# Graph attention layer: rows of 128 words in the gathered table, and the sources' part of the logits made on VectorE from the fetched rows

## What is computed

```python
xp = (x @ W).reshape(N, H, C)                      # H = 8, C = 16
a_src = jnp.einsum('nhc,hc->nh', xp, att_src)
a_dst = jnp.einsum('nhc,hc->nh', xp, att_dst)
e = leaky_relu(a_src[src] + a_dst[dst], 0.2)
m = segment_max(e, dst)
ex = exp(e - m[dst])
alpha = ex / (segment_sum(ex, dst)[dst] + 1e-16)
out = segment_sum(xp[src] * alpha[:, :, None], dst).reshape(N, 128) + bias
```

## Time and profile before

| | us |
|---|---|
| median of three runs | 10769.82 (10767.44 to 10773.94) |
| profiled execution, device time | 10778.69 |
| span of the profiled execution | 10776.9 |
| edge loop of the last layer, first to last merge (195 turns) | 2214.85 |

### The profile page before, as it was taken

The page is one execution under the profiler, slowest core; times in us unless marked ns, Lnnn a source line. Parts: engine busy times, 40 slices in busy tenths (PEclk is TensorE's granted clock), DMA queues, the critical chain, the costliest instruction groups (busy, mean ns, idle before and its releaser), DMA issues. The chain is left out here.

```text
span 10776.9 us, 275696 instructions
## 1 busy us (share of the span) xinstructions
PE 7528.6 (70%) x88315; PEld 6740.6 (63%) x88351; DVE 6269.2 (58%) x21527; ACT 2636.6 (24%) x7285; POOL 6069.2 (56%) x5927
## 2 busy tenths in 40 slices
PE   5994999997999997633333343899982566666665
PEld 4884989895898895333333333788881455555553
DVE  7995666664666666311111126677766566666666
ACT  3552222222222223200000002111111333333333
POOL 1332555552555552377777760677760777777773
PEclk7887999998999998855555566999996666666665
DMA  1005555553555555411111123333332111111113
GB/s 40 0 0 131 133 131 132 132 133 110 131 132 133 130 133 148 168 52 52 52 52 52 52 56 97 109 110 109 110 99 73 47 49 49 49 49 49 50 49 69
DMA packets 826148, 930.48 MB, mean 86 GB/s; under 512 B 135365, under 2 KB 720557, under 8 KB 825709
## 3 DMA queue, kind: packets, MB, share of 16 engines
q1 hardware_dynamic: 640390, 537.10, 17.2%
q0 software_dynamic: 185216, 386.21, 15.9%
q10 hardware_dynamic: 487, 6.55, 0.2%
HBM read 801.28 MB, written 134.46 MB: 87 GB/s over the span
## 5 line engine op out<-in xcount | busy, mean ns | idle before, releaser
L475 POOL DMA_INDIRECT ring<-att_table,idx x1592 | 1766.2, 1109 | 501.3 <-issue 455.0
L475 POOL DMA_INDIRECT ring<-rel_table,idx x1568 | 1486.5, 948 | 486.9 <-issue 477.2
L542 PE MATMUL psum<-sel,ring 128*128 128x128 f32 x3136 | 725.3, 425 | 1267.5 <-DMA ring<-rel_table,idx 1267.5
L1168 PE MATMUL psum<-state,ring 128*128 128x128 bf16 x24420 | 1511.8, 220 | 41.6 <-DVE ring L1115 34.1
L1122 DVE TENSOR_SCALAR state<-iota_row,state 128x128 f32<-128x128 f32 x5684 | 1530.1, 348 | 0.0
L542 PEld LDWEIGHTS psum<-sel,ring 128*128 128x128 f32 x3136 | 677.8, 328 | 1315.6 <-issue 1315.6
L1168 PEld LDWEIGHTS psum<-state,ring 128*128 128x128 bf16 x24420 | 1374.1, 98 | 152.2 <-issue 52.1
L1101 POOL DMA_INDIRECT ring<-gcn_table,idx x812 | 781.1, 962 | 747.9 <-ACT idx L1146 624.1
L1101 POOL DMA_INDIRECT ring<-rows,idx x812 | 781.2, 962 | 736.8 <-ACT idx L1146 612.9
L1346 POOL DMA_INDIRECT state<-hyp_table,state x980 | 962.7, 982 | 337.1 <-issue 281.3
L1182 PE MATMUL psum<-state 64*128 64x128 f32 x16240 | 1125.7, 282 | 0.3 <-DVE state L1122 0.2
(11 more groups left out here) (407 smaller groups left out, 13467.7 us busy)
## 6 DMA issues: line engine op xcount, KB each, us to landing
state<-xparts SPq DMA_DIRECT2D x814, 192.0 KB
state<-drow SPq DMA_DIRECT2D x814, 160.0 KB
rel_table<-tout SPq DMA_DIRECT2D x98, 512.0 KB, 2.6
ring<-xparts SPq DMA_DIRECT2D x199, 192.0 KB
ring<-srow SPq DMA_DIRECT2D x199, 192.0 KB
ring<-rows SPq DMA_DIRECT2D x70, 448.0 KB
ring<-att_table,idx POOLq DMA_INDIRECT x1592
ring<-rel_table,idx POOLq DMA_INDIRECT x1568
```

The costliest lines, as they stand in the source:

```text
L475: pool.indirect_dma_start(out=ring[:, u, k, 0:width], out_offset=None, in_=table, in_offset=bass.IndirectOffsetOnAxis(ap=idx[:, u, k:k + 1 ...
L542: last = nc.tensor.matmul(psum[:, u % 2, 0:WIN], ring[:, u, k, 0:D], sel[:, u % 2, k, :], start=(k == 0), stop=(k == K - 1))
L1168: last = nc.tensor.matmul(rowsP[v][:, j * P:(j + 1) * P], reach[v][:, t, j * P:(j + 1) * P], xwin[v][:, t, i, :], start=(t + i == 0), stop ...
```

## The change

The table in HBM has rows of 128 words; the stores leave the 8 logits of each row out, and a gather fetches 128 words per edge. `att_src` is loaded once more, flat and on all partitions (`att_s`), with one more DMA in the prologue. A new step on VectorE, `source_logits`, waits for the landing of a group, multiplies the 8 x 128 words per partition by `att_s` into `weighted`, waits for that product, and sums it over the 16 channels of each head into words 128 to 135 of the ring's slot. ScalarE's `stage_logits` waits for this sum (`slog`) where it waited for the landing. In VectorE's loop the step for group n+3 stands at the end of turn n, behind group_max(n+2); for groups 0, 1 and 2 it stands ahead of the loop.

```diff
-        att_table = nc.dram_tensor("att_table", (TILES * P, ROW5), F32, kind="Internal").ap()
+        att_table = nc.dram_tensor("att_table", (TILES * P, D), F32, kind="Internal").ap()
+        att_s = sb("att_s", [P, D])
+        weighted = sb("weighted", [P, K, D])
@@ prologue, sync engine (and the waits for "copied" go from 26 * 16 to 27 * 16)
+                sp.dma_start(att_s[:, :], att_src.rearrange("h c -> (h c)").partition_broadcast(P)
+                             ).then_inc(sem("copied"), 16)
@@ project, sync engine
-                                sp.dma_start(rows_of(to, b), tiles(tout[:, u, 0:BT * w], w)
+                                sp.dma_start(rows_of(to, b), tiles(tout[:, u, 0:BT * w], w)[:, :, 0:D]
@@ attention_pass
-                stage_index = gather_engines(block, att_table, srcT, ROW5, AHEAD,
+                stage_index = gather_engines(block, att_table, srcT, D, AHEAD,
@@ scalar engine (the calls lose their count in the same way)
-                    def stage_logits(n, u, count):
-                        act.wait_ge(sem(f"g{u}"), count)
+                    def stage_logits(n, u):
+                        act.wait_ge(sem("slog"), n + 1)
@@ vector engine
+                    def source_logits(n, u, landed):
+
+                        dve.wait_ge(sem(f"g{u}"), landed)
+                        if not isinstance(n, int) or n > 0:
+                            dve.wait_ge(sem("slog"), n)
+                        nc.vector.tensor_tensor(
+                            weighted[:, :, :], ring[:, u, :, 0:D], att_s[:, :].unsqueeze(1).to_broadcast([P, K, D]),
+                            ALU.mult).then_inc(sem("weighed5"), 1)
+                        dve.wait_ge(sem("weighed5"), n + 1)
+                        nc.vector.tensor_reduce(
+                            ring[:, u, :, D:ROW5], weighted[:, :, :].rearrange("p k (h c) -> p k h c", c=CH),
+                            axis=AX.X, op=ALU.add).then_inc(sem("slog"), 1)
@@ edge_logits
                         dve.wait_ge(sem("atedge"), n + 2)
+                        dve.wait_ge(sem("slog"), n + 1)
@@ ahead of the loop and at the end of each turn
+                    source_logits(0, 0, 16 * K)
                     select(0, 0)
@@
+                    source_logits(1, 1, 16 * K)
                     select(1, 1)
@@
                     group_max(1)
+                    source_logits(2, 2, 16 * K)
@@
                             group_max(n + 2)
+                            source_logits(n + 3, (u + 3) % RING,
+                                          it * (16 * K) + (16 * K if u < RING - 3 else 32 * K))
```

More of the change, by code:

```diff
@@ L213, in gnn_kernel @@
                      "ex", "msg", "summedE", "newrow", "newT", "wback",
-                     "below", "selb", "vstage", "vT", "bstage", "runmax", "runT", "runlast", "nodemax", "mg"):
+                     "below", "selb", "vstage", "weighed5", "slog", "vT", "bstage", "runmax", "runT", "runlast", "nodemax", "mg"):
             sem(name)
@@ L271, in _ @@
                 act.wait_ge(sem("load"), 12 * 16)
-                act.wait_ge(sem("copied"), 26 * 16)
+                act.wait_ge(sem("copied"), 27 * 16)
                 act.wait_ge(padded, 4 * 16)
@@ L355, in _ @@
                                           ALU.mult, ALU.add))
-                dve.wait_ge(sem("copied"), 26 * 16)
+                dve.wait_ge(sem("copied"), 27 * 16)
                 for r in range(RELS):
@@ L373, in _ @@
                 pe.wait_ge(sem("pool"), 7)
-                pe.wait_ge(sem("copied"), 26 * 16)
+                pe.wait_ge(sem("copied"), 27 * 16)
                 pe.wait_ge(sem("fin"), 1)
@@ L2235, in _ @@
                     logit_window(base_of(0))
-                    stage_logits(0, 0, 16 * K)
+                    stage_logits(0, 0)
                     starts_out(0)
@@ L2239, in _ @@
                     sel_out(0)
-                    stage_logits(1, 1, 16 * K)
+                    stage_logits(1, 1)
                     starts_out(1)
@@ L2248, in _ @@
                     sel_out(1)
-                    stage_logits(2, 2, 16 * K)
+                    stage_logits(2, 2)
                     with act.Fori(0, NG // RING) as it:
@@ L2272, in _ @@
                             sel_out(n + 2)
-                            stage_logits(n + 3, (u + 3) % RING,
-                                         it * (16 * K) + (16 * K if u < RING - 3 else 32 * K))
+                            stage_logits(n + 3, (u + 3) % RING)
                 @block.vector
```

## The result

The kernel after takes 11048.79 us (median of four runs, 11040.32 to 11062.78) against 10768.63 us: 280 us more, a ratio of 1.0261 with a 95% interval of 1.0243 to 1.0279. The profiled execution has a span of 11061.0 against 10776.9, 284 us more; at 11062.78 us it is the slowest of the four, 14 us above their median.

The account below looks back on a forecast made before the run. GpSimd, issuing gathers without a pause, bound the kernel at 11.358 us a turn. The longer ring adds 243 us and the two ends 2.5 each: 248, so 11027 us profiled, 11018 median; range 10960 to 11120.

Parts of the forecast that it names:

- Rows of 128 words cost and bring nothing: Table stores and gathers: gathers keep 0.943 us, stores gain 1.4 us at the very most, taken as 0.
- The step's own length: source_logits on VectorE: product 1.225 us, sum 1.212 us, 0.03 us ahead of each, 2.50 us together.
- The ring: Last layer's edge loop: dependences across VectorE, TensorE and ScalarE set the turn, 8.75 + 3.86 = 12.61 us against 11.358.
- the way from L2491 to L2471: From the matmuls' end through group_max, product, sum and ScalarE's copies to TensorE's turn_logits, one after the other: 3.86 us.
- the rest of the ring: Edge loop's dependent work without TensorE's wait ahead of turn_logits: 11.358 - 2.608 = 8.750 us a turn.
- TensorE's clock: Edge loop: at the 1.2 GHz level ring work is 9.13 us; all turns there would add 74 us, giving 11092.
- GpSimd second: Edge loop: GpSimd's turn 12.0 us, 0.6 below the ring's 12.61; rival that it stays last, 11095 us, chance 0.13.
- three holds of 0.68 us each: GpSimd's gathers, held under three long two-SBUF-input VectorE instructions a turn: 9.98 + 2.03 = 12.0 us.
- The ends: Outside the loop's turns: 2.5 us behind the first landing and 2.5 us ahead of the last copy.
- VectorE held in turn by a gather under way: Rival, messages and product: gathers under way block VectorE, 0.7 us a turn, 13.3 us, 11155 us; chance 0.04.
- The step hidden in TensorE's wait: Rival, edge loop: step fits TensorE's 2.608 us idle; about 10775 us, or 10900 with one more hold; chance 0.05.
- The row width as the cause of long gathers: Rival, gathers: GpSimd's floor becomes 10.0 us but the ring still gives 12.6; 10505 with a hidden step; chance 0.02.

Follow-up runs that it names:

- the second run with att_s in PSUM: The kernel after with att_s copied once to a free PSUM bank, run again off the chip that stretched every kernel: 11075.71 us, ratio 1.0266 to the kernel before.
- the step with wide rows: The kernel after with rows of 136 words stored and fetched again, the step overwriting the fetched logits: 11050.1 us, ratio 1.0262 to the kernel before.
- the early place: The kernel after with source_logits moved on VectorE from behind group_max to ahead of messages: 10823.83 us, ratio 1.0052 to the kernel before.
- select's row in PSUM: The kernel before with the row of indices that select reads copied once to a free PSUM bank: 10581.42 us, ratio 0.9825 to the kernel before.
- the kernel with both PSUM edits: The kernel before with select's row of indices and the edges' weights for messages in PSUM: 10549.09 us, ratio 0.9776 to the kernel before.
- the rows alone: The kernel before with rows of 128 words in table and gathers and no step on VectorE, output not the reference's: ratio 1.0004 to the kernel before.

## Why the prediction was right

**What bounds the kernel before.** Right: GpSimd's gathers with their holds. Taking away first select's and then both gave 1.75% and 2.24%.

**Rows of 128 words cost and bring nothing.** Right: 1.0004.

**The step's own length.** The product 1.225 us as forecast, the sum 1.220 against 1.212: 2.45 us and 0.06 for the two starts.

**The ring.** Right in mechanism: the 12.61 us forecast came out as 12.777. The difference, 0.17 us or 33 us in all, is most of the 36 us by which the 11027 for the profiled execution fell short of 11063. Half is in the way from L2491 to L2471, 3.950 us against 3.86: in half of the turns VectorE pauses 0.19 us between group_max and the product (19.5 us in 98 cases, above), which the earlier trace rows couldn't show. The other half is in the rest of the ring, 12.777 - 3.950 = 8.827 against 8.750. There I had named TensorE's clock, and the granted clock over the loop went from 0.64 to 0.59. The traces with the same ring bear it out in part. The way is the same in all, 3.95 to 3.96 us; the rest is 8.83 us at 0.59 (the kernel after), 8.75 at 0.61 (the second run with att_s in PSUM) and 8.65 at 0.63 (the step with wide rows). Turns that run at 0.50 throughout, the 1.2 GHz level, have a rest of 9.15 us on average in the kernel before and after alike, near the 9.13 of the prediction; the kernel after has 45 of them and the step with wide rows 17. So the size of the rest goes with the clock of the execution that happened to be profiled, and the 12.618 us of the step with wide rows, which fall on the forecast, owe it in part to the two errors of 0.1 us cancelling. No run sets the clock by itself.

**GpSimd second.** Right in rank: it waits for its indices, and a product that holds nothing leaves the time alone. Its turn of 8 x (1.170 + 0.305) = 11.8 us is near the 12.0 of the sum, and it idles 1.0 us a turn where I had 0.6. But three holds of 0.68 us each are not what came. Per turn the product's are worth 0.85 us, those of messages 0.84 and those of select 0.14; their sum, 1.8 us, is near the 2.03 of the forecast by luck. A held gather ends 0.8 us after VectorE's instruction, so a hold is worth anything from nothing to 1.05 us by where the gather begins under it. That didn't matter after the change, where GpSimd isn't last, and it is why the early place was better than I expected and select's row in PSUM too. The price of the sum, taken as 0, is right: in the second run with att_s in PSUM 198 gathers begin under it, half of them in its first 0.27 us, and all but one, begun in its last 0.01 us, take their usual time.

**The ends.** The first merge comes 8.1 us later. 4.1 of it arose ahead of the pass (its first gather starts at 8375.6 against 8371.5), where the change has next to nothing; the same point lies at 8396.5 in the kernel with both PSUM edits, which has nothing new there either, and between 8371.5 and 8398.7 in all undisturbed traces, so I take it for scatter. The other 3.9 are against 2.5 forecast; that the products for groups 1 and 2 add the rest is not shown. At the pass's end the forecast 2.5 us is absent. The last copy:

```profile
L2211 ACT ACTIVATE tout<-ring x199: 256/256/257, 8389.4 to 10916.0; 128x64 f32<-128x64 f32 x199
```

It starts 7.9 us after the last merge against 8.5 before (10631.80 in the earlier trace rows, the last merge at 10623.26). GpSimd is ahead there now, as in the loop, so the step takes the place of the wait for the last landing and isn't added to it.

**The rivals.** VectorE held in turn by a gather under way: no. The 199 products lie between 1.224 and 1.227 us, but only 34 of them begin under a gather. The kernel with select's row in PSUM says more: 192 of its 197 messages begin under one, last 1.224 to 1.226 us, and start 0.03 us after the weights like the others. The step hidden in TensorE's wait: that wait grew instead. The row width as the cause of long gathers: no, by the rows alone.

## What to carry to other kernels

A wait of 2.6 us on one engine is not room for 2.5 us of work on another: write down what has to follow what from the end of that wait backwards, and put the new step where its engine is idle and where what follows it on the ring has time to spare. Here the same instructions cost 2.6% behind group_max and 0.5% ahead of messages. And if GpSimd issues gathers without a rest, look first at what VectorE runs beside them: one operand moved to PSUM was worth 1.75%.

## What the runs showed of the hardware

A gather is held by one of these 128x1024 VectorE instructions with both inputs in SBUF if it begins while that one runs, and ends some 0.8 us after it: 1.97 us under the product above. An instruction of the same length with one input in PSUM holds none (0.94 us at 8609.06), nor does the reduction with its one input in SBUF (0.94 at 8610.31). A gather that began 0.07 us before such an instruction isn't held (9508.85), and VectorE's instruction is neither lengthened nor made to wait by it (192 messages of 1.224 to 1.226 us, above).

The Trainium skill ("SBUF — State Buffer", Who interferes with whom) says that on this chip a reduction never contends with GpSimd and that an instruction with two SBUF inputs does with one that reads SBUF. The trace agrees, with the 0.94 us at 8610.31 and the 1.97 us under the product. It also says that whichever of the two is issued first blocks the other. By the 192 messages VectorE isn't blocked, and the measurement decides.

The PSUM operand costs VectorE nothing here: 1.22 us for the product either way.
